# Routing stage of an attention and mixture-of-experts kernel: three parts of the chunk loop in another order

## What is computed

```python
x = x + _mla(_rmsnorm(x, g1), Wq, Wdkv, Wuk, Wuv, Wo)      # x is xn here; out @ Wo is the "projection"
t = _rmsnorm(x, g2)                                        # 8192 tokens of 256
logits = t @ gate_w                                        # 8 experts
top_v, top_i = jax.lax.top_k(logits, 2)
gates = softmax(top_v)
out = sum over the two experts e of gate_e * (silu(t @ w1[e]) @ w2[e])
```

## Time and profile before

| | |
|---|---|
| median of 3 runs | 2916.65 us (2916.34 to 2917.58) |
| the profiled execution, its time | 2925.71 us |
| its span | 2923.9 us |
| busy in the span: TensorE | 2546.4 us, 87% |
| VectorE | 2283.6 us, 78% |
| GpSimd | 2180.7 us, 75% |
| ScalarE | 1570.9 us, 54% |
| mean granted TensorE clock | 0.943 of full speed |

### The profile page before, as it was taken

How to read it: one execution, slowest core, us unless ns; L and a number is a source line. 1 busy time by engine, 2 the same in 40 slices (tenths; PEclk the granted TensorE clock), 3 DMA queues, 4 the chain that set the end, 5 groups by cost and what they waited for, 6 DMA issues and landing times. The chain is left out here.

```text
span 2923.9 us, 58265 instructions
## 1 busy us (share of the span) xinstructions
PE 2546.4 (87%) x21356; PEld 1302.0 (45%) x21356; DVE 2283.6 (78%) x3685; ACT 1570.9 (54%) x2357; POOL 2180.7 (75%) x1196
## 2 busy tenths in 40 slices
PE   7999878999999999999999999985672988898893
PEld 4544432333333333333333333224562877777782
DVE  4558758899989998999899988603653899999980
ACT  2322225777777777677777767781221544444441
POOL 4543339798889888988889888993565677778782
PEclk9999999999999999999999999996765999999996
DMA  6785642123323332333223321117864555565555
GB/s 204 255 276 195 221 160 64 48 76 87 81 63 86 86 80 65 84 85 88 60 84 85 89 59 60 43 40 237 283 208 154 120 122 121 114 138 125 124 91 149
DMA packets 252852, 351.78 MB, mean 120 GB/s; under 512 B 30536, under 2 KB 192168, under 8 KB 251816
## 3 DMA queue, kind: packets, MB, share of 16 engines
q1 hardware_dynamic: 224968, 304.32, 35.1%
q0 software_dynamic: 27360, 39.73, 7.9%
q10 hardware_dynamic: 256, 4.19, 0.4%
HBM read 255.35 MB, written 162.43 MB: 143 GB/s over the span
## 5 line engine op out<-in xcount | busy, mean ns | idle before, releaser
L1044 DVE TENSOR_REDUCE p_piece_max<-p_ring 128x1 f32<-128x512 f32 (+3 forms) x2160 | 1293.7, 655 | 137.0 <-PE p_ring L157 67.4
L1102 ACT ACTIVATE p_probs<-p_st 128x1024 f32<-128x1024 f32 (+3 forms) x1280 | 1078.8, 897 | 414.2 <-PE p_st L1165 216.7
L1165 PE MATMUL p_st<-unit_q,unit_k 64*128 64x512 bf16 (+3 forms) x3520 | 433.1, 348 | 41.6 <-ACT p_probs L1102 24.9
L1183 PE MATMUL p_pv<-p_probs,unit_vg 128*32 128x512 f32 (+3 forms) x3520 | 411.6, 542 | 0.0
L982 POOL TENSOR_TENSOR p_terms<-p_head_p,p_head_in 128x4096 f32<-128x4096 f32 x32 | 348.7, 10897 | 0.1
L1835 POOL DMA_INDIRECT acc<-p_y,p_rows x142 | 223.4, 1573 | 135.8 <-ACT p_y L1963 49.5
L170 PE MATMUL p_ring<-unit_k,unit_q 64*128 64x512 bf16 (+3 forms) x1600 | 271.6, 352 | 27.9 <-DVE p_piece_max L1044 25.4
L961 POOL TENSOR_TENSOR p_terms<-p_head_in 128x4096 f32<-128x4096 f32 x32 | 283.2, 8850 | 8.4 <-POOL p_head_s L969 4.4
L2000 PE MATMUL p_y_ps<-p_w,p_hid 128*128 128x256 f32 x1136 | 278.9, 402 | 11.1 <-ACT p_hid L1951 10.8
L1818 POOL TENSOR_TENSOR p_pv<-p_pr,p_qkv 128x1280 f32<-128x1280 f32 (+2 forms) x78 | 259.6, 3328 | 26.8 <-ACT p_q_ps L1943 26.8
L988 POOL TENSOR_TENSOR p_terms<-p_terms 128x2048 f32<-128x2048 f32 (+2 forms) x96 | 252.2, 2627 | 17.1 <-POOL p_terms L988 11.4
(11 more groups left out here) (187 smaller groups left out, 3477.4 us busy)
## 6 DMA issues: line engine op xcount, KB each, us to landing
p_w<-ffn_w SPq DMA_DIRECT2D x142, 512.0 KB
qk_parts<-p_parts SPq DMA_DIRECT2D x64, 384.0 KB, 3.4
head_qkv<-p_heads SPq DMA_DIRECT2D x16, 1536.0 KB, 6.7
p_rows<-rows_by_expert SPq DMA_DIRECT2D x71, 258.0 KB, 3.4
unit_q<-qk_parts SPq DMA_DIRECT2D x132, 128.0 KB, 3.2
unit_k<-qk_parts SPq DMA_DIRECT2D x132, 128.0 KB, 3.6
v_padded<-p_vx SPq DMA_DIRECT2D x16, 1024.0 KB, 8.2
p_head_in<-head_qkv SPq DMA_DIRECT2D x32, 384.0 KB, 3.8
```

The lines of the kernel that those rows point to most:

```text
L1044: nc.vector.tensor_reduce(piece_max[:, n % 2, h:h + heads, i, pc], ring_ps[g % RING][:, 0:heads * width].rearrange("p (h k) -> p h k", h=h ...
L1102: nc.scalar.activation(probs[:, 2 * turn_of(s, i) + u, :, 0:width], st_ps[u][:, :, 0:width], ACT.Exp).then_inc(probs_done, 1)
L1165: last = nc.tensor.matmul(st_ps[u][:, half, 0:width], k6[s][rows, PAIR * second + u, kt * P:(kt + 1) * P], q6[s][rows, PAIR * second + u, ...
L1183: last = nc.tensor.matmul(pv_ps[hh * VW:(hh + 1) * VW, skip:CT], vg[s][:, kt, hh * VW:(hh + 1) * VW], probs[:, 2 * turn_of(s, i) + hh % PA ...
```

## The change

On GpSimd the root of chunk n+2 moves from ahead of the scatters of chunk n to behind the sixth of the eight. On VectorE `add_attention(n + 2)` moves from ahead of the gates and positions of chunk n to behind them. On TensorE the projection of n+2 moves behind the transposes of n+1 and the ranks of n. No instruction is added, removed or resized.

```diff
             def body(b, c, n, ahead):
-                if ahead >= 2:
-                    inverse_rms(n + 2)
                 wait_apart(pool, th_copied, n + 1, apart)
                 wait_apart(pool, pos_done, n + 1, apart)
                 for t in range(TT):
+                    if t == TT - 1 and ahead >= 2:
+                        inverse_rms(n + 2)
                     for k in range(2):
                         nc.gpsimd.indirect_dma_start(
...
                 nc.vector.tensor_tensor(either[:, :, :], chosen[:, :, 0, :], chosen[:, :, 1, :], ALU.add
                                         ).then_inc(either_done, 1)
-                if ahead >= 2:
-                    add_attention(*after(b, c + 2), n + 2)
-
                 dve.wait_ge(ediff_done, n + 1)
...
                 nc.vector.tensor_copy(pos[:, c, :, :], pos_f[:, :, :]).then_inc(pos_done, 1)
                 assert links[0] == LINKS
                 if ahead >= 2:
+                    add_attention(*after(b, c + 2), n + 2)
                     add_x(*after(b, c + 2), n + 2)
                     scale_rms(*after(b, c + 2), n + 2)
...
             def body(b, c, n, ahead):
                 logits_of(n)
-                if ahead >= 2:
-                    project(*after(b, c + 2), n + 2)
                 if ahead >= 1:
                     transpose_th((c + 1) % NC, n + 1)
                 ranks(n)
+                if ahead >= 2:
+                    project(*after(b, c + 2), n + 2)
             chunks(pe, body)
```

## The result

The changed kernel takes 2970.12 us in the median (2966.51 to 2971.73, 4 runs) against 2916.49 us for the kernel before (4 runs). The ratio is 1.0182, with a 95% interval of 1.0165 to 1.0200: slower by 53.6 us. The forecast was 2963, with a range of 2942 to 2986.

A forecast was written before the change was run, and what follows sets the result against it. The routing stage (280 of 2923.9 us) was taken as bound by a ring of waits, not one full engine. Ten turns with jumps +44.5, then +6.6 and -4.2, gave +46.9 us: 2972.6 profiled, 2963 predicted, range 2942 to 2986.

The forecast's parts named there:

- The ring: Routing stage: position chain, cast to scatter, six scatters, root and scaling follow one another, 17.0 us a chunk against 14.06.
- The tail: Last scatter groups: chunk 13 to 14 takes 17.0 us (+6.6), chunk 14 to 15 takes 10.4 us (-4.2).
- The jumps: VectorE's loop jumps back after chunks 3 and 7: stalls of 8.15 and 6.94 us stand in full, 15.1 us.
- Rival 1: VectorE's jumps back are covered by the longer wait for the root: -15.1 us, 2948 us; chance 0.10.
- The cover for the late projection: VectorE's additions and the squares end about 12.2 us, before the root's turn at 13.7: 1.5 us to spare.
- The addition beside a scatter: VectorE's addition lengthens a GpSimd scatter from 0.96 to 1.60 us; that 0.64 lies inside the six scatters' 7.9 us.
- Rival 2: VectorE's additions hold GpSimd's scatters fully, 1.91 us per turn instead of some 0.6: +15.6 us, 2979 us; chance 0.10.
- Late ranks: VectorE's remote wait for TensorE's ranks: costed at 0 in the new order, upper end 4.4 us every second chunk.
- Rival 3: TensorE's late signals stay on the ring: +22 us, 2985, or +61 us, 3024, if the projection's are late; chance 0.10.
- Rival 4: Faster: positions come 1.80 us sooner, so GpSimd's 15.3 us of waits for them vanish, 2901 us; chance 0.06.
- Rival 5: No change: a turn of the routing stage stays near 14 us, as now; chance 0.04.
- the same difference gives 2963.5: Last step: the median lies 9 us below the profiled execution, so 2972.6 us profiled becomes a median of 2963.5.

The follow-up runs named there:

- e2: The kernel before with only GpSimd's root moved behind six scatters: 2984.94 us, ratio 1.0176.
- e7: The changed kernel with TensorE's order of before and the root behind two scatters instead of six: 2915.51 us, ratio 1.0002.
- e10: The changed kernel with TensorE's order of before and the root behind four scatters instead of six: 2935.41 us, ratio 1.0071.
- e4: The changed kernel with the chunk loop written out on every engine, so that no engine jumps back: 2954.97 us.
- e3: The changed kernel with TensorE's order of before (projection ahead of transposes and ranks): 2968.82 us.
- e5: The kernel before with only TensorE's order changed (projection behind transposes and ranks): 2959.63 us, ratio 1.0154.
- e11: The changed kernel with GpSimd's root back ahead of the scatters, the same program as e1 run again: 2945.65 us, ratio 1.0104.
- e6: The kernel before with only VectorE's order changed (additions behind the positions): 2916.58 us, ratio 1.0008.
- e0: The kernel before once more, unchanged, in another session: 2913.73 us.
- e1: The changed kernel with GpSimd's root back ahead of the scatters, first execution: 2973.56 us.

## Why the prediction was right, and where it was off

- **The ring**: right, and the main cause. 17.0 forecast for a turn, 16.81 in chunk 5. Term by term: chain 4.8 against 4.64; cast to scatter 1.0 and 0.99; six scatters 7.9 and 8.06; root 1.5 and 1.49; scaling 1.8 and 1.63. e2, e7 and e10 show it by lengthening and shortening it.
- **The start at chunk 3**: 2071.0 forecast, 2071.59 measured. Chunk 13: 2071.05 + 185.1 = 2256.2 forecast, 2255.36 measured. **The tail**: 17.0 and 10.4 forecast, 16.18 and 11.89 measured. The first scatters of chunks 3, 13, 14 and 15:

```profile
2071.59 0.96 POOL L1445 DMA_INDIRECT rows_by_expert<-p_th,p_pos  x1 [4.71 <-DVE p_pos L1541]
...
2255.36 0.96 POOL L1445 DMA_INDIRECT rows_by_expert<-p_th,p_pos  x1 [4.39 <-DVE p_pos L1541]
...
2271.54 0.96 POOL L1445 DMA_INDIRECT rows_by_expert<-p_th,p_pos  x1 [4.69 <-DVE p_pos L1541]
...
2283.43 0.96 POOL L1445 DMA_INDIRECT rows_by_expert<-p_th,p_pos  x1 [0.30 <-issue]
```

- **The jumps**: 15.1 forecast, 7.76 + 7.33 = 15.09 measured. That they stand on the ring in full is right: the scatters behind them wait that much longer than the others, and e4 loses it. Rival 1 falls. The close agreement of the size is luck. It was carried over from stalls split another way (2.84 + 5.31 and 1.28 + 5.66, now 5.20 + 2.56 and 4.63 + 2.70), and other kernels with the same jumps and the root behind six show 5.2 and 5.1 us (e2) and 6.3 and 6.1 us (e3).
- **The cover for the late projection**: right, with a margin close to the forecast. The last addition ended 10.18 us after the first copy (10.4 forecast), the last square starts at 2118.52 in chunk 5 and the root 2.4 us later without a wait. e5 and e11 show what that cover hid: with the root ahead, the projection is the next bound.
- **The addition beside a scatter**: 1.73 against 0.96 us, once a turn. Rival 2 priced 1.91 us. The attention's addition, though, ended at 2112.54, before the first scatter at 2112.73, and the larger one had 0.90 us left when its scatter began, of which 0.77 came on top. So the rule of the Trainium skill, "SBUF — State Buffer", that the prediction names is borne out as far as these rows go; the rival's price was wrong because it took whole instructions in place of what was left of them.
- **Late ranks**: costed at 0 in the new order, and 0 they are. Rival 3 falls, for this order. The reason given, that the ranks meet an idle GpSimd, is not proven by it: the ranks of chunk 15 meet a scatter group in the changed kernel and were not late either.
- **Rival 4** falls: e6, which has what it needs (positions sooner, the root ahead), gains nothing. **Rival 5** falls with the turn of 16.9.
- **The step that failed**: "the same difference gives 2963.5". In the profiled executions the difference was 2971.73 - 2925.71 = 46.0 us, against 46.9 forecast. But 2925.71 contained late ranks, which push GpSimd's scatters, and I carried the difference over to a median that by all signs lacks most of them. The changed kernel can't shed that time, since it no longer has such waits. Against e0 (no late ranks, 2913.73 us) the difference of the profiled executions is 58; between the medians it is 53.6. That the runs of the median lack the late ranks is an inference from e0, one execution of another session. I had the 9 us gap between profile and median before me, and the 27.4 us of remote waits beside it, and did not put the two together.

## What to carry to other kernels

In a software pipeline written out by hand per engine, moving one step behind others on one queue is priced by the ring it closes: follow the step's result to the engine that needs it, through that engine's own order, and back to the first instruction behind which the step now waits. If the turn is shorter than the busiest engine's share of a chunk the move is free (two scatters), above that each moved instruction counts in every turn (four, six). And before a difference is carried from a profiled execution to a median, ask which waits the profiled one has that the others may not.

## What was not expected of the hardware

VectorE's wait for the ranks can last several microseconds beyond the shown end of their matmuls, in some executions and not in others of the same program. The rank addition waits for a signal of TensorE and for one of VectorE's own; the trace names neither as what ended the wait, so that TensorE's is the late one is a reading. e1 and e11 are one program: 28.4 us of remote waits and 2973.56 us in one session, none and 2945.65 us in the other, with a granted clock of 0.937 and 0.940. The kernel before varies likewise, 2933.1 in one session and 2915 in the others. Those sessions ran on different chips, so the chip may be what differs.

In the first profile the ranks of chunk 5 end at 2094.0 and are used at 2100.63, while GpSimd is in a scatter group; where it stood idle (chunks 2, 4 and 8) there was no such wait. A scatter group is not enough for it, though: in chunks 6, 10, 12 and 13 of the same profile the ranks met one too, and the addition came without a wait about 2.1 us after them. In the five late chunks of the loop the wait ends within 0.2 us of the end of GpSimd's power instruction (2100.63 against 2099.70 + 1.04 in chunk 5), but in e1 it does not: in its chunk 5 it ends at 2110.50, in the middle of a scatter group that began at 2103.33. The changed kernel and e3, whose ranks meet an idle GpSimd in all chunks but the last, took 2970 and 2969 us in the two kinds of session. What holds VectorE back stays open; it wasn't isolated. If the kernel before had late ranks in its 2933 us session, for which there is no trace, that is also why comparing e2, e3 and e4 with it understates the cost.
